# Graph network on one core: in the message layers, waits for copied rows and added sums are moved from TensorE to VectorE, and unused rows are cleared once

## The chip, the cores and the metric

One Trainium2 chip, one core of it. The metric is the device time of one execution in microseconds (us); lower is better. The engines are named as in the profile: PE is TensorE (matmuls; PEld its weight loads), DVE is VectorE, ACT is ScalarE, POOL is GpSimd, SP is SyncE, which only issues transfers here.

## The reference, cut to what matters

A graph of 6250 nodes and 206250 edges, 128 features per node. After a normalisation, a first network runs two message layers, a second one three linear layers. The change touches only the two message layers:

```python
for l in range(2):
    m = jnp.concatenate([h[row], h[col]], axis=-1)          # two rows per edge
    m = jax.nn.relu(m @ msg_W1[l].T + msg_b1[l])
    m = m @ msg_W2[l].T + msg_b2[l]
    agg = jax.ops.segment_sum(m, col, num_segments=N)       # summed by target node
    upd = jnp.concatenate([h, agg], axis=-1) @ upd_W[l].T + upd_b[l]
    h = _layer_norm(h + upd, ln_g[l], ln_b[l])
```

The kernel applies `msg_W1` to the nodes ahead of the edges (two tables of rows, one for the source and one for the target of an edge) and `msg_W2` behind the sums, so that per edge two rows are fetched and added, a Relu is taken, and the result is added to its target node.

## The kernel before, in words

First the edges are sorted (0 to about 577 us of the span), the node tables are made, then comes message layer 1 (about 617 to 1262 us), an update stage, message layer 2 (about 1352 to 1992 us), another update stage, and three linear layers. Nodes lie in 50 tiles of 125.

**A message layer** (`cells_sp`, `cells_pe`, `cells_act`, `cells_dve`, `cells_pool`) runs over the 50 target tiles twice, once for each half of the source tiles. I call these passes loops 1 and 2 (layer 1) and loops 3 and 4 (layer 2); in the code `kk` is 0 to 3. In loops 1 and 3 a target tile takes 6 *visits*, in loops 2 and 4 it takes 7 (`VISIT`), so there are 1300 visits. A tile's visits are numbered 0 to 5 or 6; visits 0 to 2 are *part 0*, the rest are *part 1* (`part_of`). Parts have operands of their own, index 0 or 1:

- `toN[part]`: one-hot rows that pick source rows; `toB[part]`: one-hot rows that pick rows of the target tile. DVE makes both by comparing a loaded list with a column (`by_node`, L1418 and L1419). The matmul with `toB` reads 96 partitions, of which DVE writes 64 for each tile; rows 64 to 95 are unused and must be zero.
- `cur[:, part]`: the target tile's own rows, copied by ACT from a loaded buffer (`own_rows`, L1386). Rows 64 to 95 are unused too.
- `toE[part]`: one-hot columns that add messages to their nodes, made by DVE (`by_slot`, L1427).

**A visit on PE** is a `gather` (matmuls with `toN`, L1349, and with `toB` and `cur`, L1353, into a PSUM bank), and a `scatter` (`toE` times the messages, L1367, into `psA[part]`). PE's queue holds gather(pos + 2), then scatter(pos). ACT turns each gathered bank into messages (Relu, L1400). When a part's last scatter is done, DVE adds `psA[part]` to the table of sums (`sums`, L1435).

Every engine runs its queue in the order in which it is written. For one tile that is:

- ACT, `cells_act`: messages of visit 0, then `own_rows(1, ...)` for this same tile; messages of visits 1 to 3, then `own_rows(0, ...)` for the next tile; the other messages.
- DVE, `cells_dve`: `by_node` for part 1 of this tile, `sums(1)` of the tile before, `by_slot` for part 1; then `by_node` for part 0 of the next tile, `sums(0)` of this tile, `by_slot` for part 0 of the next.
- PE, `cells_pe`: the Python loop shown below; its hardware loop closes between the scatter of a tile's last visit and gather 2 of the next tile.

PE waits for semaphores: `f_toN` (both operands of `by_node` ready), `f_cur[part]` (rows copied), `f_msg` (messages ready, which also frees the PSUM bank), `f_toE`, and `f_add[part]` (sums added, so that `psA[part]` may be overwritten). `hold` is a wait that an instruction of its own carries on the engine's queue, followed by a count on another semaphore.

```python
if at in (0, 3):
    half = part_of(at)
    pe.wait_ge(f_cur[half], i + (tiles_before(kk, half == 0) + tile + 1 + half))
    pe.wait_ge(f_toN, i * 2 + part_done(kk, tile, half))
pe.wait_ge(f_msg, before_visit(i, kk, pos))
```

All these operands are carved out of one memory, the arena. In the kernel before, what the update stage between the layers writes there overlaps `toB`. The unused rows of `toB` and `cur` are cleared at the start of each message layer (L1445, counted on `f_one`, for which PE waits ahead of its first gather).

## Time and profile before

| what | us |
|---|---|
| median of 3 runs (lowest, highest) | 3299.42 (3295.45, 3306.16) |
| the profiled execution: its span | 3302.9 |
| PE busy | 2918.4 (88%) |
| DVE busy | 2503.1 (76%) |
| ACT busy | 2057.0 (62%) |
| POOL busy | 703.6 (21%) |

The profiled execution is an execution of its own. Its time is given by its span, 3302.9 us, which is 3.5 us above the median of the three runs and between their lowest and highest. Busy shares are means over stages with different limits, so a stage is read by itself. Matmuls overlap, and a matmul's end is modelled; the start of the first matmul of a group is the safer number. A bracket behind a row of the timeline gives the time for which the engine had been idle ahead of it, and what ended that.

### The profile page before, as it was taken

The page shows a single profiled execution, that of the slowest core. Times are in us where ns is not written, and L with a number is a line of the kernel's source. Part 1 is how long each engine was busy: PE and PEld are TensorE (multiplying, and loading weights), DVE is VectorE, ACT ScalarE, POOL GpSimd, SP SyncE. Part 2 cuts the span into 40 slices and gives each one's busy share as a digit, 9 for nine tenths or more (in the row PEclk, how much of TensorE's full clock was granted, in tenths as well). Part 3 has the DMA queues.
Part 4 walks back from the last instruction along what each step waited for, and adds up shares of the span by engine and source line. Part 5 has one row for each costly group of instructions (what it writes and reads, how often), then busy time and mean ns, then how long its engine had stood idle before and what let it go on. Part 6 is the DMA issues. An engine that isn't in the chain of part 4 may idle for free.

```text
span 3302.9 us, 219046 instructions
## 1 busy us (share of the span) xinstructions
PE 2918.4 (88%) x88775; PEld 2722.9 (82%) x88775; DVE 2503.1 (76%) x4764; ACT 2057.0 (62%) x3886; POOL 703.6 (21%) x909
## 2 busy tenths in 40 slices
PE   3666665799999998799999997799999899999999
PEld 3555454699989997699989996699999799999999
DVE  8999999777767776677777775689899855565555
ACT  1433333677767776777767774677777555555555
POOL 2222123400011117200011116244444300000000
PEclk7777776999999999899999998799999999999999
DMA  3000000566656762466667663155555488868888
GB/s 74 7 6 6 6 6 20 179 186 182 189 167 185 190 183 68 142 186 187 185 171 188 185 182 56 50 180 183 182 183 184 147 262 265 265 214 246 272 262 252
DMA packets 409174, 518.87 MB, mean 157 GB/s; under 512 B 157279, under 2 KB 280709, under 8 KB 409095
## 3 DMA queue, kind: packets, MB, share of 16 engines
q1 hardware_dynamic: 395757, 498.98, 51.0%
q0 software_dynamic: 4000, 8.20, 2.2%
q10 hardware_dynamic: 9338, 10.73, 1.1%
q8 instruction: 38, 0.62, 0.1%
q14 instruction: 41, 0.34, 0.0%
HBM read 408.98 MB, written 108.72 MB: 157 GB/s over the span
## 4 chain that ended last, share of the span: by engine, by line
PE 70%; DVE 13%; issue 7%; DMA 4%; POOL 3%; ACT 2%; SPq 0%; DVEq 0%; POOLq 0%; ACTq 0%
PE psum L1349 19%; PE psum L1583 17%; PE psum L1367 9%; PE psum L1353 9%; PE psum L1570 6%; PE psum L1550 3%; PE psum L703 1%; DMA tabf<-in_x 1%; PE psum L1558 1%; DMA cells_kept<-arena 1%; DVE Hf L943 1%; DVE Hf L1082 1%; DMA arena<-rows_far,ovcur 1%; DVE Hf L2144 1%; POOL arena L2057 1%
## 5 line engine op out<-in xcount | busy, mean ns | idle before, releaser
L1349 PE MATMUL psum<-tabf,arena 125*32 125x128 f16 x40256 | 1091.8, 220 | 27.9 <-DVE arena L1445 16.0
L1353 PE MATMUL psum<-arena 96*32 96x128 f16 x20928 | 1027.5, 221 | 7.4 <-issue 7.4
L1349 PEld LDWEIGHTS psum<-tabf,arena 125*32 125x32 f16 x40256 | 949.8, 98 | 91.4 <-issue 45.0
L1400 ACT ACTIVATE arena<-psum 128x512 f32<-128x512 f32 x1300 | 775.2, 596 | 340.4 <-PE psum L1353 339.5
L1353 PEld LDWEIGHTS psum<-arena 96*32 96x32 f16 x20928 | 690.5, 95 | 7.7 <-issue 7.7
L1583 PE MATMUL psum<-tabr,cellr 125*125 125x256 f32 x5000 | 623.4, 285 | 6.2 <-ACT cellr L1502 6.0
L1583 PEld LDWEIGHTS psum<-tabr,cellr 125*125 125x125 f32 x5000 | 606.4, 187 | 7.1 <-issue 7.1
L1367 PE MATMUL psum<-arena 128*32 128x129 f32 x10400 | 565.9, 277 | 1.4 <-issue 1.4
L1502 ACT CAST cellr<-arena 125x630 fp32r<-125x630 f16 x500 | 359.7, 720 | 267.4 <-PE psum L1583 255.8
L1502 DVE CAST cellr<-arena 125x630 fp32r<-125x630 f16 x500 | 244.0, 488 | 241.3 <-PE psum L1583 236.0
L1612 ACT CAST arena<-psum 125x500 f16<-125x500 f32 x625 | 356.6, 578 | 100.7 <-PE psum L1550 46.0
L1570 PE MATMUL psum<-tabf,arena 125*125 125x256 f16 x2500 | 380.2, 275 | 6.0 <-ACT arena L1612 6.0
L1435 DVE TENSOR_TENSOR AGGf<-AGGf,psum 125x129 f32 x404 | 117.1, 290 | 259.9 <-PE psum L1367 259.7
L1570 PEld LDWEIGHTS psum<-tabf,arena 125*125 125x125 f16 x2500 | 264.2, 138 | 8.4 <-ACT arena L1612 8.1
L1307 POOL COPY ovcur<-ovidx 128x1 int32 x50 | 28.4, 568 | 1126.2 <-PE psum L1353 1126.2
L1367 PEld LDWEIGHTS psum<-arena 128*32 128x32 f32 x10400 | 256.0, 110 | 11.5 <-issue 1.9
L1550 PE MATMUL psum<-arena 128*125 128x125 bf16 x2508 | 250.6, 223 | 16.5 <-DVE arena L1622 16.4
L1550 PEld LDWEIGHTS psum<-arena 128*125 128x125 bf16 x2508 | 228.5, 139 | 21.2 <-DVE arena L1622 20.0
L1386 ACT COPY arena<-tabf 64x512 f16<-64x512 f16 x402 | 243.1, 605 | 1.0 <-ACT AGGf L1875 1.0
L1427 DVE TENSOR_TENSOR arena<-col,to_slots 128x384 f32<-128x384 bf16 (+1 forms) x404 | 236.1, 584 | 0.0
L1419 DVE TENSOR_SCALAR arena<-arena,row 64x1536 f16<-64x1536 uint8 (+1 forms) x202 | 216.4, 1071 | 0.0
L1419 DVE TENSOR_SCALAR arena<-tabf,row 64x1536 f16<-64x1536 uint8 x200 | 214.3, 1071 | 0.0
(313 smaller groups left out, 4444.9 us busy)
## 6 DMA issues: line engine op xcount, KB each, us to landing
arena<-cells_kept SPq DMA_DIRECT2D x500, 315.0 KB, 3.5
cells_kept<-arena SPq DMA_DIRECT2D x625, 126.0 KB
arena<-slots_turned_from SPq DMA_DIRECT2D x152, 384.0 KB
tabf<-slots_turned_from SPq DMA_DIRECT2D x150, 384.0 KB, 4.0
arena<-slots_turned_from SPq DMA_DIRECT2D x50, 512.0 KB
tabf<-slots_turned_from SPq DMA_DIRECT2D x50, 512.0 KB
arena<-slots_turned_to SPq DMA_DIRECT2D x152, 96.0 KB
tabf<-slots_turned_to SPq DMA_DIRECT2D x150, 96.0 KB, 4.3
```

What stands on the lines that cost most here:

```text
L1349: pe.matmul(psCell[b][q:q + GW, g * D:(g + 1) * D], fr, rows, start=g == 0 and p == 0, stop=False, tile_position=(0, q), skip_group_check= ...
L1353: m = pe.matmul(psCell[b][q:q + GW, g * D:(g + 1) * D], toB[part][:, here + q:here + q + GW], cur[:, part, g, :], start=g == 0 and 4 * k + ...
L1367: m = pe.matmul(psA[half][q:q + GW, 0:W], toE[half][:, pos - 3 * half, g, :], msgs[:, SLOT[pos], g, 0:W], start=first, stop=pos == part_en ...
L1386: act.copy(cur[0:CP * GW, half], stack_in[u]).then_inc(f_cur[half], 1)
L1400: act.activation(msgs[:, SLOT[pos], :, 0:D], psCell[SLOT[pos]].rearrange("p (c d) -> p c d", d=D), ACT.Relu).then_inc(f_msg, 1)
L1419: dve.tensor_scalar(toB[half][0:CP * GW, span], slist[v][half][1][:, span], row32[:], None, ALU.is_equal).then_inc(f_toN, 1)
L1427: dve.tensor_tensor(toE[half][:, 0:count], col1[:, 0:GW].rearrange("p (o u e) -> p o u e", o=1, u=1).to_broadcast(grid), to_slots[:, :, at ...
L1502: copy(cells_r[:, q % UNIT_RING], held.rearrange("p (c e) -> p c e", c=UNIT)).then_inc(l_cast[e], 1)
L1550: m = pe.matmul(psMsg[b][0:P, c * P:(c + 1) * P], oneE[:, n % MARKS, at, 0, 0:P], oneE[:, n % MARKS, at, 1, 0:P], start=True, stop=True, s ...
L1570: m = pe.matmul(psA[u][0:P, 0:LP * D], cells[0:P, pos % RING, c, 0:P], TABL[:, t].rearrange("p c d -> p (c d)"), start=t == 0, stop=t == N ...
L1583: m = pe.matmul(psA[u][0:P, 0:2 * D], cells_r[:, q % UNIT_RING, k, 0:P], TABR[:, first + k].rearrange("p c d -> p (c d)"), start=first + k ...
L1612: act.copy(cells[0:P, pos % RING, :, 0:P], psMsg[pos % RING][0:P, 0:GROUP * P].rearrange("p (c d) -> p c d", d=P)).then_inc(l_Cc, 1)
```

## The change: what it does

1. PE no longer waits for `f_cur`. DVE waits for it instead (a `hold`) between the two instructions of `by_node`, ahead of writing `toB`, and only behind that counts `f_toN`.
2. PE no longer waits for `f_msg` ahead of a gather. The scatters in front of that gather in PE's queue have waited for later messages.
3. PE no longer waits for `f_add` ahead of a part's first scatter. DVE waits for it in `by_slot`, ahead of writing `toE`.
4. ACT copies the rows of the next tile (`own_rows(0, ...)`) behind the messages of visit 2, no longer behind those of visit 3.
5. `toE` takes the place of `toB` in the arena, `toB` moves behind everything that the update stage uses, and `cur` behind `msgs`. The three clears of unused rows are made once, in `first_dve`, ahead of the first layer, behind waits for the sort's last stores; they are gone from both layers, and PE waits for `f_one` at 4 + l.

```diff
--- before.py
+++ after.py
@@ -248,6 +248,7 @@
 
 
         arena_words = 11808
+        STAGE_USED = 2 * 2 * 128 + 3 * 2 * D + 3 * 2 * 2 * D + 3 * 2 * D
         STAGE_WORDS = PB * 2 * D * 4 + 4 * 128
         arena_at = (nc.sbuf_base + 31) // 32 * 32
         arena = sb("arena", [128, arena_words])
@@ -314,15 +315,16 @@
 
         carve = carver(arena, arena_words)
         toN = [carve([P, n * RG * CELL], F16) for n in SPAN]
+        toE = [carve([128, n, RG, GW]) for n in SPAN]
+        carve([128, STAGE_USED - sum(n * RG * CELL // 2 + n * RG * GW for n in SPAN)])
         toB = [carve([STACKED, n * RG * CELL], F16) for n in SPAN]
-        toE = [carve([128, n, RG, GW]) for n in SPAN]
-        cur = carve([STACKED, 2, RG, D], F16)
         ovrows = carve([128, CP, D], F16)
         carve = carver(arena[:, STAGE_WORDS:], arena_words - STAGE_WORDS)
         slist = [[None, None], [None, None]]
         for n in range(2):
             slist[0][n] = [carve([128, 4 * RG * CELL], F16), carve([CP * GW, RG * CELL]).bitcast(U8)]
         msgs = carve([128, CELL_RING, RG, W + 1])
+        cur = carve([STACKED, 2, RG, D], F16)
         carve = carver(tabf[:, NT * 2 * D:2 * half], 2 * half - NT * 2 * D)
         stack_in = [carve([CP * GW, RG, D], F16) for _ in range(2)]
         for n in range(2):
@@ -1326,10 +1328,7 @@
                     at, tile = pos % n, pos // n
                     if at in (0, 3):
 
-                        half = part_of(at)
-                        pe.wait_ge(f_cur[half], i + (tiles_before(kk, half == 0) + tile + 1 + half))
-                        pe.wait_ge(f_toN, i * 2 + part_done(kk, tile, half))
-                    pe.wait_ge(f_msg, before_visit(i, kk, pos))
+                        pe.wait_ge(f_toN, i * 2 + part_done(kk, tile, part_of(at)))
                     if ks[at] == SPARE:
                         pe.wait_ge(f_far, i + (l * NT + tile + 1))
                     b, k = SLOT[at], ks[at]
@@ -1361,14 +1360,13 @@
                     first = pos in (0, 3)
                     if first:
                         pe.wait_ge(f_toE, i * 2 + marks_done(kk, 0, half))
-                        pe.wait_ge(f_add[half], i + (kk * (NT + half) + 1 + half))
                     for g in range(RG):
                         q = g * GW
                         m = pe.matmul(psA[half][q:q + GW, 0:W], toE[half][:, pos - 3 * half, g, :], msgs[:, SLOT[pos], g, 0:W], start=first,
                                       stop=pos == part_end(kk, half), tile_position=(0, q), skip_group_check=True)
                     m.then_inc(f_sca, 1)
 
-                pe.wait_ge(f_one, 4 * (l + 1))
+                pe.wait_ge(f_one, 4 + l)
                 pe.wait_ge(f_msg, visit_base(kk))
                 for pos in range(2):
                     gather(0, pos)
@@ -1401,7 +1399,7 @@
                                            ).then_inc(f_msg, 1)
                             if pos == 0:
                                 own_rows(1, w, None, i * (2 * n) + visit_done(w - 1, kk, n - 1, 2))
-                            if pos == 3:
+                            if pos == 2:
                                 own_rows(0, 1 - w, i * 32 + 32 * (kk * (NT // 2) + (kk // 2 if w else 0) + 1 + w), i * (2 * n) + visit_done(w, kk, 2, 2))
 
         def cells_dve(dve, l):
@@ -1416,6 +1414,8 @@
                     dve.wait_ge(f_gat, i * (2 * n) + visit_done(w + tile - 1, kk, part_end(kk, half), 2))
                     span = slice(0, positions(kk, half) * RG * CELL)
                     dve.tensor_scalar(toN[half][:, span], slist[v][half][0][0:P, span], row1[0:P, :], None, ALU.is_equal)
+
+                    hold(dve, "dve", f_cur[half], i * 2 + (tiles_before(kk, half == 0) + w + tile + 1 + half))
                     dve.tensor_scalar(toB[half][0:CP * GW, span], slist[v][half][1][:, span], row32[:], None, ALU.is_equal).then_inc(f_toN, 1)
 
                 def by_slot(i, w, tile, half):
@@ -1424,6 +1424,7 @@
                     at = slice(w + tile, w + tile + 1) if isinstance(i, int) else bass.ds(i * 2 + (w + tile), 1)
                     k0 = HALVES[h][3 * half]
                     dve.wait_ge(f_sca, i * (2 * n) + visit_done(w + tile - 1, kk, part_end(kk, half)))
+                    dve.wait_ge(f_add[half], i * 2 + (kk * (NT + half) + w + tile + 1 + half))
                     dve.tensor_tensor(toE[half][:, 0:count], col1[:, 0:GW].rearrange("p (o u e) -> p o u e", o=1, u=1).to_broadcast(grid),
                                       to_slots[:, :, at, k0:k0 + count].rearrange("p g o k -> p (o k) g").rearrange("p k (g e) -> p k g e", e=1)
                                       .to_broadcast(grid), ALU.is_equal).then_inc(f_toE, 1)
@@ -1440,9 +1441,6 @@
                     by_node(0, 0, 0, 0)
                 dve.wait_ge(f_toE, LEAD + kk * (2 * NT + 1))
                 by_slot(0, 0, 0, 0)
-                if h == 0:
-                    for unused in (toB[0], cur, toB[1]):
-                        dve.memset(unused[CP * GW:STACKED], 0.0).then_inc(f_one, 1)
                 with dve.Fori(0, NT // 2) as i:
                     for w in range(2):
                         by_node(i, w, 0, 1)
@@ -1971,6 +1969,11 @@
         def first_dve(dve):
             dve.wait_ge(s_pset, CONSTANTS + L0 + 2)
             dve.tensor_copy(AGG[:, :, D], selfs[0:P, 1:NT + 1])
+            dve.wait_ge(o_ST, SORTS)
+            for u in range(2):
+                dve.wait_ge(o_store[u], 32 * (SORTS // 2 + 1))
+            for unused in (toB[0], toB[1], cur):
+                dve.memset(unused[CP * GW:STACKED], 0.0).then_inc(f_one, 1)
             dve.wait_ge(s_root, 1)
             dve.tensor_reduce(reach[:, 0:1], linear_bound, AX, ALU.max)
             for p in range(MULT, DUOS + MULT):
```

How this moves instructions shows best at two places. The first is PE's queue in loop 1, from the close of its hardware loop: gather 2 (its last rows), the scatter of visit 0, and the start of gather 3 (the names in brackets are semaphores: `cells_slot_onehots_ready` is `f_toE`, `cells_part_added0` is `f_add[0]`, `cells_tile_rows_copied1` is `f_cur[1]`, `cells_node_onehots_ready` is `f_toN`). Before:

```order
L1353 MATMUL psum<-arena 32x128 x4
L1359 REGISTER_ALU
L1363 ISA [waits cells_messages_ready]
L1364 REGISTER_ALU [waits cells_slot_onehots_ready]
L1367 MATMUL psum<-arena 32x129 [waits cells_part_added0]
L1367 MATMUL psum<-arena 32x129 x3
L1330 REGISTER_ALU
L1331 REGISTER_ALU [waits cells_tile_rows_copied1]
L1349 MATMUL psum<-tabf,arena 32x128 [waits cells_messages_ready,cells_node_onehots_ready]
L1349 MATMUL psum<-tabf,arena 32x128 x7
```

And with the change:

```order
L1352 MATMUL psum<-arena 32x128 x4
L1358 ISA
L1362 ISA [waits cells_messages_ready]
L1365 MATMUL psum<-arena 32x129 [waits cells_slot_onehots_ready]
L1365 MATMUL psum<-arena 32x129 x3
L1331 REGISTER_ALU
L1348 MATMUL psum<-tabf,arena 32x128 [waits cells_node_onehots_ready]
L1348 MATMUL psum<-tabf,arena 32x128 x7
```

Two register instructions and three waits are gone from this place; gather 3 is left with the wait for `f_toN` alone.

The second place is DVE's queue at the top of its hardware loop in loop 1: `by_node` for part 1 of a tile, `sums(1)`, `by_slot`. Before:

```order
L1418 TENSOR_SCALAR arena<-arena,row 125x1536 [waits cells_rows_gathered]
L1419 TENSOR_SCALAR arena<-arena,row 64x1536
L550 ISA [waits cells_messages_summed]
L1435 ISA [waits cells_part_added0]
L1435 TENSOR_TENSOR AGGf<-AGGf,psum 125x129
L1427 ISA [waits cells_messages_summed]
L1427 TENSOR_TENSOR arena<-col,to_slots 128x384
```

And with the change:

```order
L1416 TENSOR_SCALAR arena<-arena,row 125x1536 [waits cells_rows_gathered]
L552 ISA
L1419 TENSOR_SCALAR arena<-arena,row 64x1536 [waits cells_tile_rows_copied1]
L552 REGISTER_ALU [waits cells_messages_summed]
L1436 ISA [waits cells_part_added0]
L1436 TENSOR_TENSOR AGGf<-AGGf,psum 125x129
L1428 ISA [waits cells_part_added1,cells_messages_summed]
L1428 TENSOR_TENSOR arena<-col,to_slots 128x384
```

The comparison that writes `toB` (L1419 in both) now stands behind a wait for the rows that ACT copies, and the one that writes `toE` behind a wait for DVE's own addition.

## Rows read from the trace of the kernel before

**Rows 1.** View by stretches: loops 1, 2; busy us of PE, PEld, DVE, ACT, POOL, PEclk, DMA
```profile
640.00:900.00 260.00, 260.00 (x15348) 244.10 (x15344) 201.32 (x366) 200.24 (x366) 0.00 (x0) 1.00 0.63 184
940.00:1240.00 300.00, 297.81 (x17205) 280.53 (x17198) 225.35 (x359) 223.21 (x404) 39.49 (x44) 1.00 0.68 187
```

**Rows 2.** Waits in loop 1: who waited for whom, us in total, times, longest us
```profile
ACT arena L1400 <- PE psum L1353: 59.7, 182, 0.5
...
PEld psum L1349 <- issue: 8.4, 46, 0.2
```

**Rows 3.** Timeline, one tile of loop 1: start us, us, engine, line
```profile
797.62 0.30 PE L1349 MATMUL psum<-tabf,arena 125*32 125x128 f16 x8
...
798.02 0.61 DVE L1418 TENSOR_SCALAR arena<-arena,row 125x1536 f16<-125x1536 f16 x1
...
798.53 0.30 PE L1349 MATMUL psum<-tabf,arena 125*32 125x128 f16 x8
798.55 1.00 DVE L1419 TENSOR_SCALAR arena<-arena,row 64x1536 f16<-64x1536 uint8 x1
...
798.62 0.60 ACT L1400 ACTIVATE arena<-psum 128x512 f32<-128x512 f32 x1 [0.39 <-PE psum L1353]
...
799.11 0.61 ACT L1386 COPY arena<-tabf 64x512 f16<-64x512 f16 x1
...
800.10 0.29 DVE L1435 TENSOR_TENSOR AGGf<-AGGf,psum 125x129 f32 x1 [0.55 <-PE psum L1367]
...
800.26 0.43 PE L1367 MATMUL psum<-arena 128*32 128x129 f32 x8
800.30 0.55 DVE L1427 TENSOR_TENSOR arena<-col,to_slots 128x384 f32<-128x384 bf16 x1
...
800.57 0.30 PE L1349 MATMUL psum<-tabf,arena 125*32 125x128 f16 x8
```

**Rows 4.** Timeline, one tile of loop 2, rows around the copy and gather 3
```profile
1081.96 1.27 DVE L1419 TENSOR_SCALAR arena<-arena,row 64x2048 f16<-64x2048 uint8 x1
...
1082.78 0.60 ACT L1386 COPY arena<-tabf 64x512 f16<-64x512 f16 x1
...
1084.27 0.30 PE L1349 MATMUL psum<-tabf,arena 125*32 125x128 f16 x8
```

**Rows 5.** Timeline, one tile of loop 3, the copy and gather 3
```profile
1421.99 0.61 ACT L1386 COPY arena<-tabf 64x512 f16<-64x512 f16 x1
...
1423.39 0.30 PE L1349 MATMUL psum<-tabf,arena 125*32 125x128 f16 x8
```

**Rows 6.** Timeline, one tile of loop 4, the copy and gather 3
```profile
1723.57 0.60 ACT L1386 COPY arena<-tabf 64x512 f16<-64x512 f16 x1
...
1725.13 0.29 PE L1349 MATMUL psum<-tabf,arena 125*32 125x128 f16 x8
```

**Rows 7.** Timeline, the start of message layer 1
```profile
617.87 0.62 ACT L1386 COPY arena<-tabf 64x512 f16<-64x512 f16 x1 [0.64 <-ACT AGGf L1875]
...
621.50 0.91 DVE L1445 MEMSET arena<- 32x1024 uint32 x1 [0.16 <-issue]
...
622.47 0.41 PE L1349 MATMUL psum<-tabf,arena 125*32 125x128 f16 x8 [8.28 <-DVE arena L1445]
```

**Rows 8.** One line's instructions: L1445, the clears of unused rows
```profile
L1445 DVE MEMSET arena<- x6: 485/698/912, 620.1 to 1355.9; 32x768 uint32 x2, 32x512 uint32 x2, 32x1024 uint32 x2
```

**Rows 9.** Timeline of DVE ahead of the first layer
```profile
577.27 1.02 DVE L1973 COPY AGGf<-selfs 125x50 f32<-125x50 f32 x1
...
580.45 0.69 DVE L1965 TENSOR_TENSOR arena<-psum,abias 125x512 f32<-125x512 f32 x1 [1.99 <-PE psum L1828]
```

**Rows 10.** ACT's timeline at the start of layer 2
```profile
1359.73 0.60 ACT L1400 ACTIVATE arena<-psum 128x512 f32<-128x512 f32 x1 [0.18 <-PE psum L1353]
1361.01 0.60 ACT L1400 ACTIVATE arena<-psum 128x512 f32<-128x512 f32 x1 [0.68 <-PE psum L1353]
```

**Rows 11.** View by stretches: PE's granted clock at the start of layer 2
```profile
1357.00:1362.00 5.00, 5.00 (x188) 4.92 (x184) 3.10 (x6) 2.29 (x4) 0.00 (x0) 0.50 0.38 94
```

## Prediction

> **What bounds the kernel now.** I read first the view by stretches. In loop 1 PE is busy 260.00 of 260 us at a granted clock of 1.00, in loop 2 297.81 of 300; DVE and ACT are busy about 77% and 75% of both [rows 1]. Then the waits: ACT waited 59.7 us for PE's gathers, in 182 waits of at most 0.5 us; what PE waited for shows as 8.4 us of "issue" in 46 pieces, about one for each tile [rows 2]. So PE bounds the message loops and the others are led by it. But a busy PE has overlapping records, so I went to the timeline of single tiles for its small gaps and for the order of events. From one gather's first matmul to the next one's takes 0.91 us (797.62 to 798.53). Between gather 0 and gather 3 lie 2.95 us (797.62 to 800.57), 0.22 more than three such visits (2.73). The close of PE's loop lies in there, and so do the waits at the scatter of visit 0 (800.26) and at gather 3 [rows 3].
>
> The same tile shows what else hangs on gather 0. ACT starts its messages at 798.62, and copies the tile's rows (part 1 of `cur`) from 799.11 to 799.72. Meanwhile DVE starts `toB` at 798.55, 1.17 us **before** that copy ends, and is done at 799.55, 1.02 before gather 3 [rows 3]. Today copy and `toB` run side by side, and PE waits for both. The change puts one behind the other.
>
> **The waits that leave PE.** They can cost no more than that 0.22 per tile, 44 us over 200 tiles, and nothing at all if the one wait that is left costs as much as three did. The loop's close stays and must have a share; I take a half, rounded down to 0.10 per tile, 20 us [rows 3].
>
> **The wait for `cur` on DVE, part 1.** The new chain is: the copy ends; DVE's hold passes and `toB` starts; `toB` runs; PE sees `f_toN` and starts gather 3. `toB` lasts 1.00 in loop 1 [rows 3], 1.27 in loop 2 [rows 4]; by their shapes the same holds for loops 3 and 4. No row shows DVE starting behind a single hold. Two rows bound the hand-over: PE started 0.06 behind DVE's last clear (621.50 + 0.91 = 622.41 to 622.47) [rows 7], and DVE idled 0.55 ahead of `sums`, which has two holds and waited for a scatter too [rows 3]. I take 0.20, nearer the first, since here there is one hold and the copy's end is the only thing waited for. DVE to PE: 0.06 by that row, 0.09 with the load that comes ahead of a matmul; bounds 0.06 and 0.20. So gather 3 can start 0.20 + 1.00 + 0.09 = 1.29 us behind the copy's end in loops 1 and 3, 0.20 + 1.27 + 0.09 = 1.56 in loops 2 and 4. It starts now:
>
> - loop 1: 800.57 less 799.72 = 0.85, so it becomes 0.44 late [rows 3];
> - loop 2: 1084.27 less 1083.38 = 0.89, so 0.67 late [rows 4];
> - loop 3: 1423.39 less 1422.60 = 0.79, so 0.50 late [rows 5];
> - loop 4: 1725.13 less 1724.17 = 0.96, so 0.60 late [rows 6].
>
> Nothing catches this up: gather 0 of the next tile stands behind gather 3 in PE's queue, PE is full in between, and the next copy counts from that gather 0. Sum: (0.44 + 0.67 + 0.50 + 0.60) x 50 tiles = 110.5 us. The gain from the waits that leave gather 3 is not to be had beside this, since only the copy counts there now. Of the 20 us above I leave 8, 0.04 per tile, for places behind gather 3, where the loops that differ in their registers may have their share; bounds 0 and 20.
>
> **The wait for `cur` on DVE, part 0, and the copy's new place.** `toB` of part 0 is needed only at the next gather 0, three visits (2.73 us) behind gather 3. From the end of `toB` of part 1 DVE needs: `sums` 0.29, the wait for its own addition 0.2 (taken as above), `toE` 0.55, the step from `toN` to `toB` 0.53 (798.02 to 798.55), `toB` 1.00, hand-over 0.09: 2.66 against 0.09 + 2.73 = 2.82 [rows 3]. It fits by 0.16. ACT copies part 0 right behind the messages of visit 2, which by then is more than a microsecond old. It pushes the messages of visit 3 back by at most its 0.61, and their scatter stands behind gather 5. These edits cost nothing while that holds; uncovered, the first costs its excess in each tile of loops 1 and 3, 100 tiles (loops 2 and 4 have one visit more).
>
> **The wait for `f_add` on DVE** is in that 0.2. PE needs `toE` of part 1 only behind gather 5. On SP's queue the loads of later lists wait for `f_toN` and start later by the same half microsecond; they are for two tiles on, some 11 us, so that costs nothing.
>
> A page speaks against giving waits a price. The Trainium skill, "VectorE: DVE Perf Modes", section "The DRAIN you can't avoid", says that a semaphore behind each of eight VectorE copies cost nothing extra, and advises to count operations, not semaphores. By it the added waits are free and the change is the first rival below. I think the rule speaks of the semaphore and not of what it waits for; the 1.17 us above is the latter.
>
> **Clears.** PE's first gather of a layer waits for the last clear and starts at 622.47 [rows 7]; layer 2 has the same three clears, the last at 1355.9 [rows 8]. Without them: copy ends 617.87 + 0.62 = 618.49, plus 1.29 = 619.78 [rows 7]. Gain 2.7 us per layer, 5.4 in all; bounds 2.2 (the clears alone) and 3.0. Ahead of the first layer the three clears, 2.3 us (620.1 [rows 8] to 622.41), fall into a gap: DVE copies until 578.29, then waits 1.99 us for PE until 580.45 [rows 9]. 0.4 us do not fit; bounds 0 and 2.3.
>
> **Sum.** 110.5 - 8 - 5.4 + 0.4 = 97.5 us. On the profiled execution's own 3302.9 that makes 3400.4. The median of the three runs, 3299.4, is 3.5 lower than that execution, and the forecast is for a median: 3299.4 + 97.5 = **3396.9 us**.
>
> **Rivals.**
> - *Faster: the new waits are covered.* If the copy of part 1 ended at least 1.29 us (1.56 in loops 2, 4) before gather 3, `toB` would come in time and only gains stay: 20 + 5 = 25, so 3274. For it: PE is the bound and loses instructions. Against: the copy ends 0.79 to 0.96 before gather 3 in the four tiles [rows 3 to 6]. Chance 0.06.
> - *DVE becomes the bound.* It decides once three added waits eat more than the 0.16 above. At 0.4 each instead of 0.2 the excess is 0.2 to 0.3 in 100 tiles, 25 us: 3422. For it: 0.16 is little. Chance 0.08.
> - *The clock falls.* Now PE pauses 0.4 to 0.7 us in each tile. In a stretch granted 0.50, which is 1.2 GHz, messages came 1.28 us apart (1359.73, 1361.01) against 0.91 from gather to gather [rows 3, 10, 11]. A quarter of 1300 visits so: 325 x 0.37 = 120 on top, 3517. Against: the granted clock is 1.00 in loops 1 and 2, short pauses and all [rows 1]. Chance 0.03. The Trainium skill, "TensorE: Matmul & The Clock Gate", section "A second HAM failure mode: psum-queue depth-cycling", tells of a kernel whose short pauses between groups of matmuls made the clock swing; by that rule this would be the outcome.
> - *No difference.* Losses and gains cancel within 0.3%, 10 us, about what a measurement of this kernel can tell from no change. It needs gather 3 late by 0.15 or so, not 0.55. Chance 0.03.
>
> **How the numbers follow.** The forecast has 0.80. Its own bounds: with the first hand-over at 0.06 the sum falls by 0.14 x 200 = 28, and with all 20 us of the waits instead of 8 by 12 more: 3357. With the hand-over at 0.38, midway between 0.20 and its upper bound, it rises by 36: 3433, which takes in the DVE case. Range 3357 to 3433; left out are faster, same and the clock, 0.12, and hand-overs near the upper bound. Slower 0.80 + 0.08 + 0.03 = 0.91, same 0.03, faster 0.06.
>
> **What would show it.** In the changed profile: `toB` of part 1 starts about 0.2 behind the copy's end, and DVE's idle time there ends by ACT's copy; PE waits for DVE's `toB` about once a tile, some 100 us in all; a tile of loop 1 grows from 5.68 us (6 x 0.91 + 0.22) to about 6.1; PE's first gather of a layer starts 1.9 us behind the start of ACT's first copy, no longer 4.6. If `toB` starts late but gather 3 does not move, the slack was misread; if both move and the time doesn't, PE catches up behind gather 3. A time under 3330 makes the prediction wrong in its mechanism, one over 3433 in a size.

## The result and the profile after

| | before | after |
|---|---|---|
| median (lowest, highest), 4 runs each | 3297.43 (3295.36, 3306.16) | 3390.37 (3389.03, 3392.84) |
| ratio, 95% interval | 1 | 1.0264 [1.0248, 1.0280] |
| profiled execution, span | 3302.9 | 3387.7 |
| PE, DVE, ACT busy | 88%, 76%, 62% | 87%, 75%, 61% |

The changed kernel is 92.9 us slower by the medians and 84.8 by the spans (the profiled execution of the kernel before is the slowest of its four). Its 3390.4 us are 6.5 below the forecast of 3396.9. The busy share of each engine fell. So something waits, and the waits say what. In loop 1 of the changed kernel (who waited for whom, us in total, times, longest us):

```profile
DVE arena L1419 <- ACT arena L1384: 40.4, 43, 1.0
PEld psum L1348 <- DVE arena L1419: 23.3, 43, 0.6
DVE arena L1428 <- DVE AGGf L1436: 19.2, 86, 0.2
PE psum L1348 <- DVE arena L1419: 11.7, 43, 0.3
PEld psum L1348 <- issue: 2.2, 13, 0.2
```

43 tiles of about 6 us fill the 260 us of this view, and each has one wait of DVE's `toB` (L1419) for ACT's copy (L1384), and one of PE's gather for that `toB`. Neither was there before: the waits of the kernel before in this stretch have no such entry. The third row is the added wait of `by_slot` for DVE's own addition, 0.22 us, twice a tile. One tile of the changed kernel in order of time (start us, us, engine, line; in brackets the idle time ahead and what ended it):

```profile
798.66 0.61 DVE L1416 TENSOR_SCALAR arena<-tabf,row 125x1536 f16<-125x1536 f16 x1
798.93 0.60 ACT L1398 ACTIVATE arena<-psum 128x512 f32<-128x512 f32 x1 [0.32 <-PE psum L1352]
799.43 0.61 ACT L1384 COPY arena<-tabf 64x512 f16<-64x512 f16 x1
800.19 1.01 DVE L1419 TENSOR_SCALAR arena<-tabf,row 64x1536 f16<-64x1536 uint8 x1 [0.92 <-ACT arena L1384]
800.61 0.41 PE L1365 MATMUL psum<-arena 128*32 128x129 f32 x8
801.26 0.30 PE L1348 MATMUL psum<-tabf,arena 125*32 125x128 f16 x8 [0.23 <-DVE arena L1419]
801.62 0.56 DVE L1428 TENSOR_TENSOR arena<-col,to_slots 128x384 f32<-128x384 bf16 x1 [0.22 <-DVE AGGf L1436]
802.62 1.01 DVE L1419 TENSOR_SCALAR arena<-arena,row 64x1536 f16<-64x1536 uint8 x1
```

DVE is done with `toN` at 799.27 and stands until the copy has ended (800.04). `toB` starts 0.15 behind that, ends at 801.20, and gather 3 starts at 801.26. In the tile of before the same `toB` had started 1.17 us before the copy ended and was done 0.17 before that end [rows 3]. The last row is `toB` of part 0: it waits for nothing. The chain of work that decides the time, followed back from the last instruction, runs through the same three in this tile (start us, us, what):

```profile
799.43 0.61 ACT arena L1384
...
800.19 1.02 DVE arena L1419
...
801.26 0.30 PE psum L1348 x8
```

In loop 2 it is the same, with the longer `toB`:

```profile
1009.20 1.33 DVE L1419 TENSOR_SCALAR arena<-arena,row 64x2048 f16<-64x2048 uint8 x1 [1.49 <-ACT arena L1384]
1012.02 1.01 DVE L1419 TENSOR_SCALAR arena<-tabf,row 64x1536 f16<-64x1536 uint8 x1
```

The view by stretches of the changed kernel, in the columns of [rows 1]: the same 260 and 300 us hold 5.6% and 7.7% fewer matmuls, at a granted clock of 1.00 as before.

```profile
640.00:900.00 260.00, 248.33 (x14495) 229.43 (x14488) 199.12 (x345) 193.73 (x345) 0.00 (x0) 1.00 0.61 174
940.00:1240.00 300.00, 277.69 (x15882) 259.48 (x15877) 214.94 (x329) 209.97 (x372) 31.76 (x41) 1.00 0.60 170
```

Over the whole execution the page's costliest groups (x count | busy us, mean ns | idle time ahead, and what ended most of it) have 245 us of DVE's idle time ahead of `toB` (two rows, 127.5 and 117.3, one for each of the two buffers that the lists are loaded into; some of the second is put down to "issue") and, on PE's side, 83 us of matmuls and 126 us of weight loads (the two overlap) ahead of the gather:

```profile
L1348 PE MATMUL psum<-tabf,arena 125*32 125x128 f16 x40256 | 1092.6, 220 | 89.1 <-DVE arena L1419 83.1
L1348 PEld LDWEIGHTS psum<-tabf,arena 125*32 125x32 f16 x40256 | 942.3, 98 | 182.0 <-DVE arena L1419 126.0
L1419 DVE TENSOR_SCALAR arena<-tabf,row 64x1536 f16<-64x1536 uint8 x200 | 215.0, 1075 | 127.5 <-ACT arena L1384 127.4
L1419 DVE TENSOR_SCALAR arena<-arena,row 64x1536 f16<-64x1536 uint8 (+1 forms) x202 | 220.0, 1089 | 117.3 <-ACT arena L1384 73.9
```

The start of layer 1 got shorter. The first gather starts 1.94 us behind the start of ACT's first copy, 4.60 before [rows 7]:

```profile
613.94 0.62 ACT L1384 COPY arena<-tabf 64x512 f16<-64x512 f16 x1 [1.47 <-issue]
615.88 0.40 PE L1348 MATMUL psum<-tabf,arena 125*32 125x128 f16 x8 [6.17 <-DVE arena L1419]
```

### The profile page after: what moved, and what is told of

The parts are those of the page before. It is cut to its first block, busy times and chain, and to the rows that moved or that the text cites. A ratio compares the mean times of both kernels' runs of the same rounds, so it can differ in the third digit from the quotient of the medians.

```text
span 3387.7 us, 218617 instructions
## 1 busy us (share of the span) xinstructions
PE 2938.0 (87%) x88775; PEld 2724.2 (80%) x88775; DVE 2536.1 (75%) x4761; ACT 2078.5 (61%) x3886; POOL 694.7 (21%) x909
## 4 chain that ended last, share of the span: by engine, by line
PE 58%; DVE 18%; issue 11%; ACT 6%; DMA 4%; POOL 3%; SPq 1%; DVEq 0%; ACTq 0%; POOLq 0%
PE psum L1581 17%; PE psum L1348 14%; PE psum L1352 7%; DVE arena L1419 6%; PE psum L1568 6%; PE psum L1365 5%; PE psum L1548 3%; ACT arena L1384 3%; PE psum L705 2%; DMA cells_kept<-arena 2%; DMA tabf<-in_x 1%; PE psum L1556 1%; DVE Hf L945 1%; PE psum L702 1%; DVE AGGf L990 1%
## 5 line engine op out<-in xcount | busy, mean ns | idle before, releaser
L1352 PEld LDWEIGHTS psum<-arena 96*32 96x32 f16 x20928 | 666.1, 95 | 10.0 <-issue 9.9
L1365 PE MATMUL psum<-arena 128*32 128x129 f32 x10400 | 551.3, 275 | 2.1 <-issue 2.1
L1419 DVE TENSOR_SCALAR arena<-tabf,row 64x1536 f16<-64x1536 uint8 x200 | 215.0, 1075 | 127.5 <-ACT arena L1384 127.4
L1419 DVE TENSOR_SCALAR arena<-arena,row 64x1536 f16<-64x1536 uint8 (+1 forms) x202 | 220.0, 1089 | 117.3 <-ACT arena L1384 73.9
L1384 ACT COPY arena<-tabf 64x512 f16<-64x512 f16 x402 | 243.0, 605 | 1.8 <-issue 1.5
L1620 DVE TENSOR_TENSOR arena<-col,arena 128x2016 bf16<-128x2016 bf16 x151 | 191.0, 1265 | 26.0 <-POOL arena L1508 14.6
```

Of the source, the lines that this page charges most:

```text
L1352: m = pe.matmul(psCell[b][q:q + GW, g * D:(g + 1) * D], toB[part][:, here + q:here + q + GW], cur[:, part, g, :], start=g == 0 and 4 * k + ...
L1365: m = pe.matmul(psA[half][q:q + GW, 0:W], toE[half][:, pos - 3 * half, g, :], msgs[:, SLOT[pos], g, 0:W], start=first, stop=pos == part_en ...
L1384: act.copy(cur[0:CP * GW, half], stack_in[u]).then_inc(f_cur[half], 1)
L1419: dve.tensor_scalar(toB[half][0:CP * GW, span], slist[v][half][1][:, span], row32[:], None, ALU.is_equal).then_inc(f_toN, 1)
```

## The experiments

The first comparison is above. Eleven more kernels, and the changed kernel once more, ran on two chips, on which the kernel before took 3339.2 us (A) and 3300.3 us (B). So each is judged by its ratio to the kernel before on its own chip, and "-28 us" means against that. Two things are missing: the changed kernel was not run on chip A, and no trace of the kernel before was kept there. Where a kernel of chip A is set beside the changed one, it is by the time of a tile, and "clears alone" stands in for the kernel before on A, since the two take the same time there.

"Tile" is the time of one tile, from the number of messages that ACT makes in a stretch: for loop 1, 250 us (640 to 890) x 6 / count, for loop 2, 240 us (960 to 1200, for "copy 0 behind visit 3", whose loop 2 begins later, 1000 to 1240) x 7 / count. The rows behind the first two lines, of the kernel before and of the changed one:

```profile
L1400 ACT ACTIVATE arena<-psum 128x512 f32<-128x512 f32 x264 | 157.4, 596 | 57.6 <-PE psum L1353 57.6
```

```profile
L1398 ACT ACTIVATE arena<-psum 128x512 f32<-128x512 f32 x249 | 149.1, 599 | 64.1 <-PE psum L1352 64.1
```

| kernel | chip | median us | ratio [95%] | loop 1: count, tile | loop 2: count, tile |
|---|---|---|---|---|---|
| before | first | 3297.43 | 1 | 264, 5.68 | 252, 6.67 |
| changed | first | 3390.37 | 1.0264 [1.0248, 1.0280] | 249, 6.02 | 232, 7.24 |
| changed, again | B | 3387.56 | 1.0258 [1.0244, 1.0272] | 249, 6.02 | 232, 7.24 |
| rows waited for on PE | A | 3310.35 | 0.9917 [0.9900, 0.9934] | 270, 5.56 | 244, 6.89 |
| part 1 alone on PE | A | 3312.93 | 0.9924 [0.9907, 0.9941] | 269, 5.58 | 245, 6.86 |
| sums waited for on PE | A | 3401.31 | 1.0194 [1.0174, 1.0214] | 247, 6.07 | 230, 7.30 |
| copy 0 behind visit 3 | A | 3458.97 | 1.0361 [1.0344, 1.0378] | 230, 6.52 | 226, 7.43 |
| copy 1 first | A | 3352.20 | 1.0043 [1.0029, 1.0057] | 270, 5.56 | 230, 7.30 |
| clears alone | A | 3339.39 | 1.0002 [0.9991, 1.0013] | 263, 5.70 | 240, 7.00 |
| before without `f_msg` wait | A | 3330.83 | 0.9975 [0.9965, 0.9985] | 268, 5.60 | 240, 7.00 |
| rows on PE, copy 1 first | A | 3333.92 | 0.9984 [0.9975, 0.9993] | 271, 5.54 | 236, 7.12 |
| copy 1 first, far rows early | B | 3274.54 | 0.9921 [0.9907, 0.9934] | 271, 5.54 | 257, 6.54 |
| rows on PE, far rows early | B | 3272.72 | 0.9910 [0.9893, 0.9927] | 270, 5.56 | 256, 6.56 |
| all three | B | 3325.76 | 1.0072 [1.0058, 1.0085] | 270, 5.56 | 239, 7.03 |

### Is it the wait for the copied rows?

The changed kernel with the waits for `f_cur` of both parts back on PE:

```diff
-                        pe.wait_ge(f_toN, i * 2 + part_done(kk, tile, part_of(at)))
+                        half = part_of(at)
+                        pe.wait_ge(f_cur[half], i + (tiles_before(kk, half == 0) + tile + 1 + half))
+                        pe.wait_ge(f_toN, i * 2 + part_done(kk, tile, half))
...
-                    hold(dve, "dve", f_cur[half], ...)
```

> The changed kernel with only the wait for the copied rows moved back from VectorE to TensorE; the waits for messages and for added sums, the clears and the copy's new place stay as changed. Theory (copy of part 1 and then toB in one chain, about 2.0 us of ACT and DVE work behind gather 0): the whole loss of about 100 us goes, the gains stay (5 us of clears, 8 to 20 us of removed waits), so 3272 to 3286 us against 3297 before and 3390 changed. Rival (the wait for added sums on VectorE, the operands' new places or ACT's earlier copy of part 0 cost it): it stays above 3350 us. Rival (the wait on TensorE has its price only because it stood with others there): it ends at or above 3297 us.

Measured: ratio 0.9917 [0.9900, 0.9934], -28.8 us, on a chip where the kernel before needs 42 us more. Expected were 11 to 25 us less than before, ratios 0.9924 to 0.9967, so the gain is at or a little over the upper end of that. The tile of loop 1 falls to 5.56, below the 5.68 of before. The waits of loop 1 have no entry for ACT's copy or for `toB` any more, and PE's own "issue" gaps are nearly gone:

```profile
DVE arena L1428 <- DVE AGGf L1436: 14.0, 70, 0.2
DVE AGGf L1436 <- issue: 12.8, 48, 0.3
DVE AGGf L1436 <- PE psum L1367: 10.5, 23, 0.5
PEld psum L1350 <- issue: 1.0, 6, 0.2
```

The rest of the change is worth 0.8%, and this one wait turned it into a loss of 2.6%.

### Which part's wait?

Only part 1 goes back to PE; DVE holds for part 0:

```diff
+                        if half:
+                            pe.wait_ge(f_cur[half], ...)
...
+                    if half == 0:
                         hold(dve, "dve", f_cur[half], ...)
```

> The changed kernel with the wait for the copied rows back on TensorE for part 1 alone; for part 0 it stays on VectorE. Theory: part 0's rows are copied early enough, their toB is needed only about 3.6 us behind gather 2 and done 3.2 us behind it, so this ends within 5 us of the kernel with both parts' waits on TensorE, 3272 to 3290 us. Rival (part 0's wait has a share of the loss, as the sum of 2.66 against 2.82 us left room for): 20 us or more above that kernel.

Measured, as expected: 2.6 us above the kernel with both on PE, and the intervals overlap. Part 0's wait is covered as long as ACT copies behind visit 2; part 1's is the whole loss, as far as these runs can tell.

### Does the wait for the added sums count?

```diff
+                        pe.wait_ge(f_add[half], i + (kk * (NT + half) + 1 + half))
...
-                    dve.wait_ge(f_add[half], ...)
```

> The changed kernel with only the wait for added sums moved back from VectorE to TensorE. Theory: it lies beside the chain of gather 0, copy, toB and gather 3, so 3390 us within 8. Rival (DVE's queue is the bound in loops 1 and 3, where 0.15 to 0.23 us of this wait stand in it twice a tile): 20 to 40 us less, 3350 to 3370 us.

Measured: with this wait back on PE the tile of loop 1 is 6.07, with it on DVE 6.02; nothing is gained. DVE's 0.22 us, twice a tile, come off, and the wait for the copy takes most of them: 1.28 us ahead of `toB` in place of 0.92.

```profile
802.68 1.01 DVE L1420 TENSOR_SCALAR arena<-tabf,row 64x1536 f16<-64x1536 uint8 x1 [1.28 <-ACT arena L1385]
```

So DVE was not what bounds the changed kernel. The time, 3401 us, lies above the 3390 within 8 that were expected, but it is of chip A, where the changed kernel was not run. The verdict rests on the tiles and on this row.

### A dose: copy 0 later

The changed kernel with part 0's copy where it was before, behind visit 3:

```diff
-                            if pos == 2:
+                            if pos == 3:
                                 own_rows(0, 1 - w, ...)
```

> The changed kernel with ACT's copy for part 0 back behind the messages of visit 3. Theory: this makes a second chain of the same kind: gather 3, its messages 0.92 us behind its start, the copy from 0.49 to 1.09 behind these, 0.16 to toB, 1.00, 0.05 to gather 0: 3.2 us where three visits take 2.73, so 0.5 us late in the 100 tiles of loops 1 and 3, nothing in loops 2 and 4 with their fourth visit (3.6): 50 us more, 3430 to 3450 us. Rival (gather 0 has slack enough, or only part 1 matters): 3390 us within 10.

Measured: 6.52 us a tile in loop 1 in place of 6.02, +0.50 as expected; 3459 us in all, 9 above the range expected. DVE's timeline of this kernel shows the second wait per tile; before it, `toB` of part 0 had none:

```profile
799.50 1.01 DVE L1419 TENSOR_SCALAR arena<-tabf,row 64x1536 f16<-64x1536 uint8 x1 [0.70 <-ACT arena L1384]
802.75 1.01 DVE L1419 TENSOR_SCALAR arena<-tabf,row 64x1536 f16<-64x1536 uint8 x1 [0.73 <-ACT arena L1384]
```

In loop 2, which has a visit more to cover the wait, every second tile kept its 7.25 us; the other grew to 7.62 us, which was not expected and was not taken apart. Without its point 4, the earlier copy, the change's point 1 would cost a second time.

### The other cure: the copy earlier, the waits where the change puts them

ACT copies part 1 ahead of the messages of visit 0, no longer behind them; all waits stay as changed:

```diff
+                            if pos == 0:
+                                own_rows(1, w, None, ...)
                             act.wait_ge(f_gat, i * (2 * n) + visit_done(w, kk, pos, 2))
...
-                            if pos == 0:
-                                own_rows(1, w, None, ...)
```

> The changed kernel, all waits where the change put them; only ACT copies the rows of part 1 ahead of the messages of visit 0, right behind the messages of the tile before. Theory: the loss is the place of the copy behind gather 0 and not the wait on VectorE. The copy then ends about a visit (0.9 us) earlier or more, gather 3 was 0.4 to 0.65 us late, so nothing is late any more: 3272 to 3290 us. Rival (a wait on VectorE costs by itself, wherever the copy is): 3350 us or more.

Most of it came, not all: 1.0043 in place of the changed kernel's 1.0264, where about 0.995 was expected. In loop 1 the tile is 5.56, the same as with the waits on PE, though the waits stand on DVE: what counts is when the copy ends, not which engine waits. DVE waits 4.3 us for it there in all, no longer 40.4, and no PE wait for `toB` is left:

```profile
DVE arena L1428 <- DVE AGGf L1436: 21.0, 94, 0.2
DVE AGGf L1436 <- issue: 4.6, 23, 0.2
DVE arena L1419 <- ACT arena L1384: 4.3, 23, 0.2
PEld psum L1348 <- issue: 1.3, 8, 0.2
```

In loops 2 and 4 the expectation failed. Every second tile shrank to 6.39 us and the other grew to 8.26 in the median. From 940 to 1200 us a wait shows that in the kernel before was small (2.7 us on the weight loads, 6 times, from 960 to 1200): PE waits for rows that POOL fetches once for two tiles (`f_far`, counted at L1320).

```profile
PEld psum L1348 <- POOLq L1320: 24.0, 18, 2.2
PE psum L1348 <- POOLq L1320: 19.1, 18, 1.9
```

POOL may start that fetch only when PE's last gather of the pair before is done. From there to its count passed, in the median of this stretch, 5.6 us in the kernel before, 5.2 to 5.5 in the two traces of the changed one, 7.2 here, and the gather that needs it comes six visits later, some 5.6 us. In the changed kernel the slower tiles cover it. Of the 1.6 us more here, 0.6 are POOL's issue of the transfer (1.80 us, 1.21 before) and 1.0 the time from its end to the count (3.8, 2.8 before).

### Taking the pieces of the gain apart

The kernel before with point 5 of the change, the clears made once and the operands' new places that this needs, and nothing else:

```diff
-                if h == 0:
-                    for unused in (toB[0], cur, toB[1]):
-                        dve.memset(unused[CP * GW:STACKED], 0.0).then_inc(f_one, 1)
...
+            for unused in (toB[0], toB[1], cur):
+                dve.memset(unused[CP * GW:STACKED], 0.0).then_inc(f_one, 1)
```

> The kernel before with only the operands' new places and the clears made once. Theory: 2.7 us per layer less, 0.4 us more ahead of layer 1: 3292 us against 3297, within 3. Rival (the new places slow the comparisons: toB of 2048 elements takes 1.33 us in the changed kernel, 1.27 before): toB is as long as in the changed kernel here too, and the time at or above 3297 us.

Measured: 1.0002 [0.9991, 1.0013]. The start did shrink, to 1.81 us from copy to gather (before 4.60), and the same in layer 2, but the 5 us expected of it are not in the time; the interval leaves them out. The new places don't slow the comparison: `toB` of 2048 elements takes 1.27 us here as before. What takes the 5 us back is open.

```profile
620.12 0.62 ACT L1388 COPY arena<-tabf 64x512 f16<-64x512 f16 x1 [0.36 <-ACT AGGf L1874]
621.93 0.40 PE L1351 MATMUL psum<-tabf,arena 125*32 125x128 f16 x8 [5.49 <-DVE arena L1421]
```

The kernel before without PE's wait for `f_msg` ahead of a gather:

```diff
-                    pe.wait_ge(f_msg, before_visit(i, kk, pos))
```

> The kernel before with only TensorE's wait for messages ahead of each gather taken away; the scatters ahead of it in the queue have waited for later messages. Theory: these waits cost only where others stand beside them, ahead of gather 3 and gather 0, so 0 to 10 us less, 3288 to 3298 us. Rival (each of 1300 waits costs a few hundredths on TensorE, which is the bound): 20 us or more, below 3278 us.

Measured: -8.4 us, 0.9975 [0.9965, 0.9985], in the range expected. In loop 1 the small "issue" gaps of the weight loads fell from 8.1 us in 44 pieces (the kernel before on the first chip, 640 to 890) to these, and the tile is 5.60 against 5.70 in "clears alone" on the same chip:

```profile
PEld psum L1348 <- issue: 0.8, 5, 0.2
```

In loop 2 the tile is 7.00 in both, so the gain isn't the same in all loops.

"Rows waited for on PE" differs from "clears alone" by the waits for messages and sums that leave PE and by the copy's new place, and is 29.0 us shorter on the same chip (the interval of its ratio is 6 us either way). If 5 us are taken off its -28.8 for the starts instead, 24 are left. So these waits, with the copy's new place, are worth 24 to 29 us, 8 of them the wait for messages.

### Both cures together

> The changed kernel with the wait for the copied rows back on TensorE and ACT's copy of part 1 ahead of the messages of visit 0. Theory: both cures do the same, so the two together give no more than one: 3272 to 3290 us, within 5 us of either.

Missed: rows on PE and copy 1 first were to be within 5 us of either, and are 24 us above rows on PE alone (0.9984), and PE waits for the far rows again in loop 2 (from 1000 to 1240):

```profile
PEld psum L1350 <- POOLq L1320: 7.8, 12, 1.4
```

From POOL's release to the count passed 6.8 us here. So that fetch, not the wait for the copied rows, is what holds up a faster tile there.

### The far rows a step earlier

POOL copies the index and holds for it ahead of its wait for PE's gathers, not behind:

```diff
+                hold(pool, "pool", f_gat, t * (2 * VISIT[1]) + ...)
                 pool.indirect_dma_start(ovrows...
...
-                hold(pool, "pool", f_gat, i * (2 * VISIT[1]) + ...)
                 far_rows(i)
```

With copy 1 first and the waits as changed:

> The kernel with ACT's copy of part 1 first (all waits where the change put them), and in loops 2 and 4 POOL's copy of the index of the far rows ahead of its wait for the gathers, which is 1.4 us off the way from the last gather of a pair of tiles to the arrival of the far rows. Theory: with the chain over the copy gone, each second tile of loops 2 and 4 waited for these rows (8.2 us a tile against 6.4); with them 1.4 us sooner most of that goes: 60 to 90 us less than 3352, so 3262 to 3292 us. Rival (the second tiles are slow for another reason, such as PE's pauses while POOL issues that transfer): 3335 us or more.

Measured: 0.9921, 3274.5 us: the changed kernel's waits cost nothing once ACT copies early and the far rows keep up. On the same chip the changed kernel took 3387.6. The time is in the range expected, but not by the reason given. The edit was to take 1.4 us off the way; from POOL's release to the start of the issue it took off 0.8 (1.58 to 0.75). From the release to the count passed 4.4 us in place of 7.2 in "copy 1 first"; the other 2.0 us are a shorter issue (0.97 in place of 1.80) and a faster landing (2.7 in place of 3.8), for which no edit aimed, and the chip is another one too. With rows on PE instead:

> The kernel with the wait for copied rows back on TensorE, with POOL's copy of the index ahead of its wait as well. Theory: there PE never waited for the far rows (it paused 0.69 us once in two tiles while POOL issued the transfer, at whatever instruction it had reached), so the order on POOL changes nothing: 3305 to 3315 us. Rival (the pause is a wait for the far rows in another guise): 25 us less, 3285 us.

Measured: 0.9910, 3272.7 us, the shortest of all, 1% under the kernel before and 3.4% under the changed one. The number expected, 3305 to 3315, was for the speed of chip A, and the rival's 3285 too; by ratio it is as the same kernel without POOL's edit on chip A (0.9917), as the theory said. The trace has a reason: the issue grew from 1.21 to 2.04 us and used up the 0.8 that the edit saved, so the count came 5.6 us behind the release, as before. Whether PE's pause on chip A was a wait for the far rows, the rival, this run can't tell, since chip B has no such pause. With all three:

> Wait for copied rows back on TensorE, ACT's copy of part 1 first, and POOL's copy of the index ahead of its wait. Theory: as with the waits on VectorE, since with the copy first neither place of the wait is late: within 10 us of that kernel, 3260 to 3292 us, and under 3310.

Missed: 1.0072, and the wait for far rows is back, with 6.6 us from release to count. Two kernels with the same POOL code differ twofold in how long POOL takes to issue the transfer, from 940 to 1200 us, here copy 1 first, and then rows on PE:

```profile
L1312 POOL DMA_INDIRECT arena<-rows_far,ovcur x20 | 19.4, 972 | 168.4 <-PE psum L1352 168.4
```

```profile
L1312 POOL DMA_INDIRECT arena<-rows_far,ovcur x20 | 40.8, 2040 | 150.3 <-PE psum L1354 150.3
```

The second of them is the faster kernel, so the issue alone doesn't decide. In "all three" the issue takes 2.04 us and then the rows take 3.8 us to be counted, where most kernels have 2.7 to 2.9. That longer landing is also in "copy 1 first" (3.8) and in "both cures" (4.0), but not in "copy 1 first, far rows early" (2.7). What makes it is open; no run took it apart. What the five kernels do show is the sum: PE waited for far rows in the three with 6.6 to 7.2 us from release to count in loop 2, and did not in the two with 4.4 and 5.6.

Last, the changed kernel again. It was meant for chip A, beside the experiments there, but ran on chip B:

> The changed kernel once more, beside the kernel before in the same runs as the experiments, where the kernel before takes 3339 us. Theory: a tile's time in loops 1 to 4 is set by the chain over the copy and toB, so the tiles last 6.04, 7.24, 6.04, 7.28 us as they did, and the 1.2% by which the kernel before is slower here is partly hidden: ratio 1.018 to 1.026. If it comes out at 3401 us, the wait for added sums costs nothing on VectorE; at 3425 us it costs 25.

Measured: 1.0258 and the same tiles (6.04, 7.24, 6.03 and 7.28 us in loops 1 to 4). The loss repeats. What the sums' wait costs on chip A, which this run was to settle, it can't say.

## Why the prediction was right, point by point

- **The copy and `toB` now stand one behind the other, and gather 3 is late.** Right. The late starts were put at 0.44, 0.67, 0.50 and 0.60 us for loops 1 to 4. The mean tiles, without the first and last few of each loop, grew by 0.34, 0.53, 0.39 and 0.56 us, 91 us over 200 tiles, where the prediction had 110.5 less 8. Its sum of 97.5 stands against 92.9 by medians and 84.8 by spans.
- **The hand-over from ACT to DVE** was taken as 0.20 and is 0.15 (800.04 to 800.19). That is 9 us. It was nearer its lower bound than thought: the row of `sums` that set the upper bound of 0.55 waited for a scatter too.
- **DVE to PE** was taken as 0.09 and is 0.05 to 0.06 (801.20 to 801.26), 7 us. The row of the clears had said 0.06.
- **The length of `toB`** was taken as 1.27 in loops 2 and 4 and 1.00 in loops 1 and 3; in the medians it is 1.28, 1.31 and 1.01. That gives 3 us back. These three sizes, -9, -7 and +3, take 102.5 to 89.5, against the 91 measured.
- **The waits that leave PE** were put at 20 us at most, 8 of them returned. With the copy's new place they are worth 24 to 29 ("rows waited for on PE"), more than the 20, which was half of what one tile showed. How much came back in the changed kernel can't be told from the rest; the 8 were a guess, and no run tests them.
- **Part 0, the copy's new place, the wait for sums.** Right: nothing lost (the runs with part 1 alone and with the sums on PE). The margin of 0.16 us held, and the idle time ahead of `toE` is 0.22 or 0.16 us where 0.2 was taken. Copy 0 a visit later uses that margin up and costs 0.50 in each tile of loop 1 ("copy 0 behind visit 3").
- **The clears.** Right at the place, 2.7 us at each layer's start, but not in the time: "clears alone" shows a net gain of 0 where the sum has 5. That term of the sum isn't shown. That the clears cost 0.4 ahead of the first layer could not be seen: the first copy of layer 1 starts at 613.9 to 620.4 us in the kernels that have them there, and at 617.9 in the kernel before.
- **How much of the nearness was luck.** The mechanism is shown term by term, but that 97.5 came within 5 us of 92.9 owes something to errors of both signs: the hand-overs taken 16 us too long, `toB` 3 too short, 8 and 5 us taken off that no run confirms.
- **The rivals.** "Covered" fell with the bracket of 0.92 us ahead of `toB`. It is what "copy 1 first" builds in loop 1, where it comes true. "DVE becomes the bound" fell with "sums waited for on PE". "The clock falls" fell with the granted clock of 1.00 in both stretches: pauses of 0.2 to 0.6 us in each tile did not lower it. The Trainium skill, "TensorE: Matmul & The Clock Gate", section "A second HAM failure mode: psum-queue depth-cycling", tells of a kernel whose clock such pauses made swing; this trace does not show that.
- **The rule on semaphores** in the Trainium skill, "VectorE: DVE Perf Modes", section "The DRAIN you can't avoid", says that a semaphore behind each of eight copies cost nothing extra; by it the waits would be free. For a wait whose condition has long been met, the runs agree in the kernel's time (part 0: 2.6 us, within the intervals). For one that has not, the trace decides: some 245 us of DVE's time and 92 us of the kernel's. Nor is the wait for DVE's own addition free in DVE's time: from the start of the addition to that of `toE` passed 0.21 us before and 0.51 after (medians, 640 to 900). It was covered here.

What the prediction did not see was the neighbour: at the speed of before, the far rows of loops 2 and 4 had no margin. It did not matter to the changed kernel, whose tiles are slower, but it decides what a cure is worth.

## What to carry to other kernels

Before a wait is moved off the busiest engine, look in one tile for what stands behind it in its new queue: the wait for copied rows cost nothing on PE, where it stood ahead of the last user, and 0.3 to 0.6 us a tile on DVE, where it stood ahead of one more operation on the way to that user. The price is (end of the awaited work) + hand-over + the operation behind the wait, less the time at which the user would start anyway. If it is positive, either let the user wait, or start the awaited work earlier, and then look for the next transfer that was sized for the old pace.

## What the runs showed of the hardware that was not expected

- POOL's issue of the same indirect transfer took 0.97, 1.21, 1.80 or 2.04 us, by kernel and nearly constant within most. In the medians it grows with the time that it lies beside DVE's `toB`: 0.31 us beside it at 0.97, 0.36 at 1.21, 0.95 at 1.80, 1.19 at 2.04; "copy 1 first, far rows early" (0.47 us beside it, 0.97) is out of line. A longer issue lies beside more for its length alone, so these rows don't say which is the cause. The Trainium skill, "GPSIMD Engine Reference", section "1. Specifications", says that GpSimd's SBUF interfaces are shared with VectorE, with contention when a VectorE instruction is in a 2-port mode or has two SBUF inputs. The rows may fit that, but no run here shows the mode of `toB` or turned the overlap on and off alone.
- On chip A the PE of loops 2 and 4 pauses once for two tiles in the middle of a gather, with nothing that it waits for, while or just after POOL issues. It is shown below in the kernel with rows on PE. The kernel before on the first chip and the two fastest on chip B have no such gap. The tile of loop 2 in "clears alone" is 7.00 there against 6.67 on the first chip; 0.33 x 100 tiles makes 33 of the 42 us that separate the chips. Why one chip does this is open, and whether the kernel before does it there too is inferred, since it has no trace.

```profile
1106.02 1.21 POOL L1311 DMA_INDIRECT arena<-rows_far,ovcur  x1 [0.78 <-POOL ovcur L1309]
...
1107.34 0.22 PE L1354 MATMUL psum<-arena 96*32 96x128 f16 x1 [0.49 <-issue]
```

- The hand-over between engines is short and steady: 0.15 us from the end of ACT's copy to DVE through a hold, 0.05 from DVE to PE, 0.16 to 0.23 us from the end of DVE's own addition to `toE` behind it.
